# Clearing a part's semaphores by runs of neighbouring numbers in a decoder layer on one core

## The reference

```python
x = _layernorm(x + mamba(x))            # in_proj, conv, selective scan, gate, out_proj
x = _layernorm(x + attention(x, ctx))   # 16 query heads, 4 key/value heads of 96, keys from ctx and x
x = _layernorm(x + feed_forward(x))     # silu(x @ w1.T) * (x @ w3.T), then @ w2.T, 3584 wide

# selective scan, per step
h = exp(dt_t[..., None] * A) * h + dt_t[..., None] * B_t[:, None, :] * x_t[..., None]
y = einsum('bdn,bn->bd', h, C_t)
```

## Time and profile before

| what | value |
|---|---|
| median of 3 runs | 3204.12 us (3202.51 to 3208.49) |
| the profiled execution's own time | 3204.36 us |
| its span, first to last instruction | 3203.1 us |
| mean granted clock of TensorE | 0.95 of full |
| TensorE matmul busy | 2875.4 us (90%) |
| VectorE busy | 2425.1 us (76%) |
| GpSimd busy | 1707.6 us (53%) |
| ScalarE busy | 1590.8 us (50%) |
| moved by DMA | 434.32 MB, mean 136 GB/s |

### The profile page before, as it was taken

How to read it: one execution, slowest core, us unless ns; L and a number is a source line. 1 busy time by engine, 2 the same in 40 slices (tenths; PEclk the granted TensorE clock), 3 DMA queues, 4 the chain that set the end, 5 groups by cost and what they waited for, 6 DMA issues and landing times. The chain is left out here.

```text
span 3203.1 us, 36062 instructions
## 1 busy us (share of the span) xinstructions
PE 2875.4 (90%) x12072; PEld 2065.7 (64%) x12072; DVE 2425.1 (76%) x2167; ACT 1590.8 (50%) x2698; POOL 1707.6 (53%) x947
## 2 busy tenths in 40 slices
PE   8996487778778699999999999998879999999996
PEld 7871133333333288787888888876758888887884
DVE  6659999999999845713677777754788888885566
ACT  4448455555555443311888888873333333333443
POOL 0004999999999632500888888870124444430023
PEclk9995689999999899999999999999989999999998
DMA  3228765655665385232111111006316545557663
GB/s 145 92 86 271 230 164 133 168 148 126 160 153 145 90 287 194 75 121 83 48 35 35 35 35 36 21 13 238 108 68 215 196 171 172 180 198 250 196 186 114
DMA packets 213627, 434.32 MB, mean 136 GB/s; under 512 B 33741, under 2 KB 45773, under 8 KB 212365
## 3 DMA queue, kind: packets, MB, share of 16 engines
q1 hardware_dynamic: 195022, 420.10, 42.1%
q10 hardware_dynamic: 18432, 12.06, 1.4%
HBM read 304.02 MB, written 128.06 MB: 135 GB/s over the span
## 5 line engine op out<-in xcount | busy, mean ns | idle before, releaser
L1689 POOL TENSOR_TENSOR at_p_lo<-at_p,at_p_hi 128x512 fp32r<-128x512 f32 x384 | 512.7, 1341 | 271.5 <-ACT at_p_hi L1601 257.9
L591 POOL TENSOR_TENSOR scan_dbx<-scan_u,scan_b_bc 128x1024 f32<-128x1024 f32 x256 | 595.2, 2359 | 0.0
L723 ACT ACTIVATE mamba_ps<-scan_dt,scan_a_neg 128x512 f32<-128x512 f32 (+1 forms) x512 | 331.7, 680 | 263.7 <-DVE scan_g L737 258.2
L748 DVE TENSOR_TENSOR_SCAN mamba_ps<-mamba_ps,scan_dbx 128x1024 f32<-128x1024 f32 x192 | 432.7, 2282 | 3.3 <-ACT mamba_ps L725 2.1
L1628 DVE TENSOR_REDUCE at_neg_max<-heads_ps 128x1 fp32r<-128x1536 f32 x128 | 225.0, 1758 | 144.9 <-PE heads_ps L1699 143.0
L96 PE MATMUL ff_ps<-ff_x_hi,ff_w_hi 128*128 128x512 f32 x784 | 310.2, 396 | 17.3 <-DVE ff_u L2276 7.1
L839 PE MATMUL mamba_ps<-scan_g,scan_sel 128*32 128x512 f32 x1024 | 151.7, 664 | 181.2 <-DVE scan_g L737 168.1
L97 PE MATMUL ff_ps<-ff_x_lo,ff_w_hi 128*128 128x512 f32 x784 | 308.3, 393 | 0.0
L98 PE MATMUL ff_ps<-ff_x_hi,ff_w_lo 128*128 128x512 f32 x784 | 308.1, 393 | 0.0
L1597 ACT ACTIVATE at_p<-heads_ps 128x512 f32<-128x512 f32 x384 | 228.3, 595 | 120.7 <-PE heads_ps L1723 96.2
L2494 POOL TENSOR_TENSOR ff_raw<-ff_raw,ff_scale 128x2048 f32<-128x2048 f32 x28 | 101.3, 3617 | 349.7 <-DMA ff_raw<-in_w 349.7
(11 more groups left out here) (279 smaller groups left out, 7210.1 us busy)
## 6 DMA issues: line engine op xcount, KB each, us to landing
scan_dt<-dt SPq DMA_DIRECT2D x120, 256.0 KB, 4.7
scan_u<-u SPq DMA_DIRECT2D x120, 256.0 KB, 7.6
ff_raw<-in_w SPq DMA_DIRECT2D x56, 512.0 KB, 4.6
ff_down_ar<-ac SPq DMA_DIRECT2D x98, 256.0 KB, 2.8
ff_down_hr<-hc SPq DMA_DIRECT2D x98, 256.0 KB, 2.7
mid_first_w<-in_w_out SPq DMA_DIRECT2D x32, 512.0 KB, 5.2
ff_act_w<-in_w SPq DMA_DIRECT2D x14, 1024.0 KB, 7.6
hc<-ff_act_t SPq DMA_DIRECT2D x56, 256.0 KB, 6.2
```

Of the source, the lines that this page charges most:

```text
L591: nc.gpsimd.tensor_tensor(dbx[n % SL][:].rearrange("p (h l) -> p h l", h=2), u[it % 2][:, c:c + 2], b_bc[b][:, k // 2].unsqueeze(1).to_bro ...
L723: nc.scalar.activation(at[:, h * L + h:(h + 1) * L], dt[it % 2][:, c, h:L], ACT.Exp, scale=a_neg[:, it % IT, e:e + 1]).then_inc(a_ready, 1)
L748: nc.vector.tensor_tensor_scan(out[:], ps_a[n % SA], dbx[n % SL][:], 0.0, ALU.mult, ALU.add).then_inc(scanned, 1)
L1689: nc.gpsimd.tensor_tensor(p_lo[n % NSL][:], p[n % NSL][:], f32(p_hi[n % NSL][:]), ALU.subtract).then_inc(p_lo_done, 1)
```

## The change

`Phase.release` sorts the part's semaphore numbers, cuts them into runs of neighbouring numbers, and gives SyncE one clear instruction for each run. Then it gives all numbers back as before.

```diff
--- before.py
+++ after.py
@@ -63,8 +63,14 @@
         return self.sems[-1]
 
     def release(self):
+        left = sorted(s.num for s in self.sems)
+        while left:
+            n = 1
+            while n < len(left) and left[n] == left[0] + n:
+                n += 1
+            self.nc.sync.sem_clear(range(left[0], left[0] + n))
+            left = left[n:]
         for s in self.sems:
-            self.nc.sync.sem_clear(s)
             self.nc.release_semaphore(s)
         self.banks.close()
```

## The result

Median 3194.66 us of 15 runs (one of them, at 3418.56 us and a mean clock of 0.814, is left out of the comparison), against 3202.89 us for the kernel before in 15 runs: ratio 0.997, 95% interval 0.9962 to 0.9977. By the ratio that is 9.6 us less, between 7.4 and 12.2; the two medians lie 8.2 us apart. The forecast was 10.92 us less, 3193.4 us.

What follows compares the result with a forecast made beforehand. TensorE was busy 90% of the span, but the change touched only SyncE's queue, so place decided: 7.08 + 2.35 + 1.49 = 10.92 us off 3204.36 us gives 3193.4 us, range 3189 to 3199 us.

Steps and rivals of the forecast that it cites:

- The end: After the last barrier SyncE alone clears, nothing hides it: 121 clears become 3, 118 fewer by 60 ns, 7.08 us off.
- The first boundary: Between first and second part, 42 clears become 1 ahead of the first load: 41 by 57.4 ns, 2.35 us off.
- The whole part moves forward: Second part: everything starts earlier by the clears removed ahead of its first load, 2.35 us.
- The table load: ScalarE's load at the start of the second part, the one competitor to the clears: ends at 1107.39 us, no cover.
- the gate tile: Second part: tile ScalarE waits for until 1111.81 us; would land some 2.35 us earlier, at 1109.4 us.
- The second boundary: Between second and third part, 27 clears become 1 ahead of a transfer-bound stretch: 26 by 57.3 ns, 1.49 us off.
- The early releases: Inside scan and attention, 54 clears become 1 and 55 become 2: covered by SyncE's slack, costed at 0.
- a run costs what one costs: All merged clears: lower bound taken, one number's 25 to 49 ns; upper bound 57 to 60 ns per number, nothing saved.
- Rival 1: All merged clears: cleared number by number, only gaps go, 5.3 us saved, 3198.8 us; full step 3204.4 us; chance 0.10.
- rival 2: Both part boundaries: something unseen, such as an instruction fetch, absorbs the gain; only the end counts, 3197.3 us; chance 0.09.
- Rival 3: Earlier start meets TensorE's clock in another phase, decided at 2264 to 2400 us: slower, 3213.9 us if trebled; chance 0.03.
- Parts of equal length within 3 us: Sign of being wrong altogether: parts between the barriers differing in length from before by more than 3 us.

Runs made afterwards that it cites:

- the long series: Kernel before, with the single clears at the end of the program gone through five times (605 for 121): 3233.3 us against 3204.58, ratio 1.0097.
- the fivefold list: Kernel before, single clears made five times: at the program's end 3233.3 us (the sense under "The end"), or after the first two parts 3221.8 us (used elsewhere).
- merged early: Kernel before, with runs merged only at the two releases inside the scan and the attention (54 become 1, 55 become 2): 3204.05 us, ratio 1.0002.
- early five times: Kernel before, with single clears made five times at the two releases inside the scan and the attention: 3204.32 us, ratio 1.0002.
- the second profile of the same kernel: Profile from repeating the whole change on the same chip as its three parts, against the kernel before: median 3193.58 us, ratio 0.9969.

## Why the prediction was right

**The end, 7.08 us**: 6.9 by the trace. The step of 60 ns was right (60.4 in the long series); the 0.2 us are the three merged clears, which last 113, 78 and 79 ns in place of 30. The kernel merged at the end alone measured 5.1 us, with 6.9 inside its interval, and the fivefold list 29.2 us by its trace and 28.7 by the medians for a working of 29.0.

**The first boundary, 2.35 us**: 2.26 by the trace, for the same reason (103 ns in place of 28). "The whole part moves forward" held for the first matmul. Between the two profiles it moved by 3.2 us against the table load, more than the clears, but that is the scatter of the first transfers: in the five profiled kernels with 42 single clears here it stands 13.5, 12.9, 12.9, 12.3 and 12.2 us behind the table load (before, merged at the end, merged early, early five times, end five times), in the four with one merged clear and nothing added ahead of the first load 10.2 to 10.3 us; the means differ by 2.5 us. The slow third issue has no part in it: the fivefold list has none, and its matmul follows the first load as closely (10.3 us) as with the change. The table load stayed clear of the path, as forecast: it ends at 1104.53 us, the gate tile is there at 1108.12. But the gate tile, which the prediction had 2.35 us earlier, came only 0.8 us earlier against the table load (4.87 us behind it in place of 5.70), and it is not what the part waits for: the weight tile lands last, 3.2 us earlier. The argument named the wrong one of the three loads.

**The second boundary, 1.49 us**: 1.43 by the trace. The long transfer behind it kept its length (13.57 us for 13.87), and so the argument that a stretch limited by transfers moves with its first issue stood.

**The early releases, 0**: 1.0002 in both directions, merged and made five times, known to some 2 us by the first and 4 by the second.

**The sum, 10.92 us**: 10.6 by the traces of the two profiles, 9.6 and 9.9 us by two sets of runs. The 0.3 us are the one step that was mis-sized, "a run costs what one costs": a run of 21 to 54 numbers lasts 58 to 128 ns. Rival 1, a run cleared number by number, was right in kind and far off in size: 1.6 ns a number, where it was priced at 25 to 30. The forecast took the lower of two bounds with no row of a run of several numbers; that it came so close there was a choice that turned out well, not something its rows showed.

**The rivals.** The boundaries are not absorbed (rival 2): merging them alone gave 3.2 us, lengthening them fivefold 17.2 us by the medians for a working of 15.9, which the interval (13.8 to 24.7 us) holds and which excludes the 12.1 us of rival 2; the working was 1.2 us short of the trace since it took 57.5 ns a step where the added clears took 62. But something like the fetch that rival 2 named exists in all likelihood, and was hidden by the clears. Rival 3, another phase of the clock, got no support from starts moved by 4 and by 17 us: the mean clock of the stretch that it named, 100 us into the third part, is 0.91 before, in both profiles of the change and in the fivefold list. By the figure of the Trainium skill (Runtime: NRT & Kernel Launch, The ~15µs preamble/postamble breakdown) the time would have been an estimated 3199.0 us. A single clear costs 60 ns here, not 29, and both medians of the change are under 3195 us; but the section prices the reset at the end of a launch, not a kernel's own clears.

**What the prediction said would be seen.** Eight clears, three of them last: yes. Each near 30 ns: no. The first load at 1106.2 us: it came at 1103.39, and the first matmul at 1113.53 instead of 1117.3, as the first part was 2.9 us shorter in that execution. The distances from the barrier, not the absolute times, were the thing to forecast. Parts of equal length within 3 us: yes, 2.9, 2.1 and 2.2, all of one sign, the scatter between executions. That it held is luck: in the second profile of the same kernel the third part is 5.7 us longer than before, so 3 us was too narrow for a sign of being wrong.

## What to carry to other kernels

Price an instruction by the step from one start to the next, not by its duration: here 60 ns for an instruction of 30. Then ask of each place whether anybody else has work: the same clears are worth their full price behind a barrier or at the end of the program, and nothing in a queue that is ahead. Where the expected gain is of the size of the runs' scatter, multiply the suspected cost by five in one place at a time; the fivefold lists came out within a tenth of their working by the medians and within about a fifth by the ratios, where the runs of the change alone gave the sum to a quarter.

## What the runs showed of the hardware that was not expected

- One clear of a run lasts 30 ns for one number, 39 ns for 8, and from there 1.6 ns more for each further number (103 for 48, 113 for 54).
- Behind the barrier of the first part SyncE's issue of transfers is held once, until some 2 to 3 us after the barrier (an issue takes 0.91 to 2.0 us in place of 0.42), unless SyncE is still busy with something else: 42 single clears hid it, 24 nearly all of it. The trace's instruction queues are moving packets then. Behind the second barrier there is neither a hold nor a packet. The Trainium skill (Runtime: NRT & Kernel Launch, Instruction fetch mechanics) says that a taken branch to a page outside the present window waits for its fetch. The order of instructions has a branch into the next block right at this place, but the timeline agrees only in part: the first two loads behind the branch are issued without delay, and the third one waits. No run here took the branch away.
- The executions of the kernel before differ by 12 us (3198.67 to 3210.99), more than the whole change is worth, and the time goes with TensorE's mean granted clock, 1.8 us for each 0.001 of it.
